# One graph-transformer layer: first loads in another order, query loads placed earlier, other orders in the last group and the last chunk

## What is computed

```python
def _decomp(x, nt, w_comp, w_basis):
    W = (w_comp @ w_basis).reshape(T, x.shape[-1], -1)
    return jnp.einsum('ni,tio->tno', x, W)[nt, jnp.arange(x.shape[0])]
k, q, v = (_decomp(node_feat, node_type, wc, wb).reshape(n, H, DK) for wc, wb in ...)
kt = jnp.einsum('nhi,thij->tnhj', k, relation_att)[edge_type, src]
e = (q[dst] * kt).sum(-1) * relation_pri[edge_type] * scale
m = jax.ops.segment_max(e, dst, num_segments=n)
ex = jnp.exp(e - m[dst])
a = ex / jax.ops.segment_sum(ex, dst, num_segments=n)[dst]
vt = jnp.einsum('nhi,thij->tnhj', v, relation_msg)[edge_type, src]
agg = jax.ops.segment_sum(a[..., None] * vt, dst, num_segments=n).reshape(n, DH)
out = jax.nn.relu(_decomp(agg, node_type, w_comp_a, w_basis_a) + node_feat @ loop_weight + bias)
result = _layernorm(x + out)
```

## Time and profile before

| | us |
|---|---|
| median of 3 runs | 2042.28 |
| the runs | 2038.15 to 2045.23 |
| the profiled execution, its own time | 2054.15 |
| its span, first to last instruction | 2052.3 |
| TensorE busy | 1223.7 |
| VectorE busy | 1005.0 |
| POOL busy | 888.9 |
| ACT busy | 789.1 |

### The profile page before, as it was taken

How to read it: one execution, slowest core, us unless ns; L and a number is a source line. 1 busy time by engine, 2 the same in 40 slices (tenths; PEclk the granted TensorE clock), 3 DMA queues, 4 the chain that set the end, 5 groups by cost and what they waited for, 6 DMA issues and landing times.

```text
span 2052.3 us, 30216 instructions
## 1 busy us (share of the span) xinstructions
PE 1223.7 (60%) x6847; PEld 1015.7 (49%) x6848; DVE 1005.0 (49%) x2888; ACT 789.1 (38%) x2216; POOL 888.9 (43%) x927
## 2 busy tenths in 40 slices
PE   6999428565545555455564565555555455554788
PEld 3445215454445445455454554444544455444678
DVE  5866216444534445344453444434444344453777
ACT  4667216433333333333333333333333333333233
POOL 2781650444454444544445444354443544445000
PEclk9999759666777766777667667667776666667789
DMA  7787530222232222322223222232222322223113
GB/s 228 303 301 313 175 91 12 69 68 75 65 86 73 69 71 63 86 72 67 75 63 85 74 61 77 63 88 67 70 72 65 88 74 61 75 67 85 38 48 106
DMA packets 110628, 194.47 MB, mean 95 GB/s; under 512 B 24345, under 2 KB 76404, under 8 KB 104188
## 3 DMA queue, kind: packets, MB, share of 16 engines
q0 software_dynamic: 41680, 113.71, 19.6%
q1 hardware_dynamic: 66380, 79.10, 11.0%
q10 hardware_dynamic: 2400, 0.07, 0.1%
HBM read 134.12 MB, written 59.48 MB: 94 GB/s over the span
## 4 chain that ended last, share of the span: by engine, by line
another core or an unknown queue 30%; PE 26%; DVE 16%; issue 15%; DVEq 9%; ACT 2%; DMA 1%; ACTq 1%
PE pb L1703 6%; DVE agg L742 5%; PE pb L1651 4%; DVEq L713 4%; PE pb L1538 3%; DVE work L707 3%; PE pb L1813 2%; PE pb L1559 2%; PE pb L1678 2%; PE pb L1609 1%; DVE work L599 1%; PE pb L1640 1%; DVE work L609 1%; DVEq L582 1%
## 5 line engine op out<-in xcount | busy, mean ns | idle before, releaser
L1223 POOL DMA_INDIRECT kv<-table,idx_now x832 | 788.0, 947 | 935.0 <-DVE work L707 645.3
L742 DVE TENSOR_TENSOR agg<-agg,pb 128x136 f32 x832 | 241.8, 291 | 801.5 <-remote 613.8
L1703 PE MATMUL pb<-work,onehot 128*128 128x136 f32 x1664 | 391.6, 377 | 353.4 <-DVE agg L742 225.2
L1703 PEld LDWEIGHTS pb<-work,onehot 128*128 128x128 f32 x1664 | 327.0, 270 | 386.1 <-issue 244.9
L1365 ACT ACTIVATE work<-pb 128x512 f32<-128x512 f32 x208 | 123.9, 596 | 818.9 <-remote 636.6
L1651 PE MATMUL pb<-q_all,work 128*128 x1664 | 313.1, 351 | 0.1
L1651 PEld LDWEIGHTS pb<-q_all,work 128*128 128x128 f32 x1664 | 296.3, 265 | 3.7 <-issue 3.0
L1640 PE MATMUL pb<-ident,onehot 128*128 128x128 f32 x832 | 181.1, 357 | 184.3 <-ACT onehot L1359 99.9
L1352 ACT ACTIVATE work<-lane,neg_lane 128x128 f32<-128x128 f32 x800 | 252.9, 389 | 0.0
L1640 PEld LDWEIGHTS pb<-ident,onehot 128*128 128x128 f32 x832 | 127.6, 184 | 209.6 <-ACT onehot L1359 116.1
L599 DVE TENSOR_TENSOR work<-kv,pb 128x512 f32<-128x512 f32 x208 | 141.9, 682 | 22.0 <-issue 12.0
(11 more groups left out here) (202 smaller groups left out, 1291.4 us busy)
## 6 DMA issues: line engine op xcount, KB each, us to landing
table<-kv SPq DMA_DIRECT2D x49, 1024.0 KB, 4.7
kv<-table,idx_now POOLq DMA_INDIRECT x832
seg<-item_bias SPq DMA_DIRECT2D x52, 64.0 KB
kv<-base_rows SPq DMA_DIRECT2D x7, 448.0 KB, 4.5
kv<-in_x_dram SPq DMA_DIRECT2D x8, 384.0 KB, 5.7
pair<-in_x_dram SPq DMA_DIRECT2D x24, 128.0 KB
base_rows<-pair SPq DMA_DIRECT2D x24, 128.0 KB
onehot<-in_x_dram SPq DMA_DIRECT2D x7, 384.0 KB
```

Source lines behind the costliest of these rows:

```text
L742: v.tensor_tensor(a, a, PB[banks[i // 2 % len(banks)]][:, (i % 2) * 256:(i % 2) * 256 + W], ALU.add).then_inc(s_added, 1)
L1223: pool.indirect_dma_start(out=kv[:, o:o + 2 * D], out_offset=None, in_=table, in_offset=bass.IndirectOffsetOnAxis(ap=idx_now[par][:, i:i + ...
L1703: mm = t_.matmul(PB[banks[k % len(banks)]][:, u * 256:u * 256 + W], onehot[:, o:o + P], wv[:, b % WR, h * 2 + u, :], start=True, stop=True)
```

## The change

- Head: the basis `basis_k` is issued right behind the first chunk of x, `basis_v` as ACT's first transfer. The 8 strips of priorities become one load of all 64 to every partition (`pri_all`), from which VectorE takes each partition's own head by a product with a mask (`own_head`, made by POOL in three steps) and a reduce. POOL copies `src` and `edge_type` only after `dst` has landed and both bases have.
- Table stage: `STARTS_AT` 8 to 9, `COLUMNS_AT` one block later each, `QUERIES_AT` 45 to 41.
- Last group: each step of the maxima ahead of two old additions, and `weigh` in four steps of one item, one behind each addition.
- Last chunk: three parts of 4, 2 and 1 blocks, each with its own residual, statistics, root and reciprocal; ACT normalises the first six blocks and VectorE the last; the output goes in three stores; the last block's product lies in a bank of its own; the root of the chunk before comes one copy earlier on ACT.

```diff
-        TILES_AT, STARTS_AT, BIAS_AT, QUERIES_AT = 4, 8, 24, BLOCKS - 4
-        COLUMNS_AT = [12, 13, 15, 16, 18, 19, 20]
+        TILES_AT, STARTS_AT, BIAS_AT, QUERIES_AT = 4, 9, 24, BLOCKS - 8
+        COLUMNS_AT = [13, 14, 16, 17, 19, 20, 21]
...
-        SPLIT = 4
+        LAST_PARTS = ((0, 4), (4, 6), (6, CB))
...
+        def last_out(c, n):
+            if c == CB - 1:
+                return PB[6][:, 0:D]
+            return PB[4 + c // 4][:, c % 4 * D:(c % 4 + n) * D]
...
             def scale_relations():
-                dve.wait_ge(s_relations_loaded, 16 * 3 * H)
+                dve.wait_ge(s_own_head, 3)
+                dve.wait_ge(s_relations_loaded, 16 * (2 * H + 1))
+                p3 = pri_all.rearrange("p (t h) -> p t h", t=T)
+                did(v.tensor_tensor(p3, p3, own_head.unsqueeze(1).broadcast_to([P, T, H]), ALU.mult))
+                did(v.tensor_reduce(pri, p3, AX.X, ALU.add))
...
+            def weigh_item(g, par, b, u):
+                if u == 0:
+                    dve.wait_ge(s_weights, g * NBATCH + wave_of[b][1] + 1)
+                rows = rows_of(par, b)[:, u, D:2 * D]
+                ins = v.tensor_tensor(wv[:, b % WR, u, 0:D].rearrange("p (h k) -> p h k", h=H),
+                                      rows.rearrange("p (h k) -> p h k", h=H),
+                                      weights_of(b)[:, u, :].unsqueeze(2).broadcast_to([P, H, DK]), ALU.mult)
+                if u == 3:
+                    ins.then_inc(s_weighted, 1)
...
             for k, steps in enumerate(maxima(g, 1, GROUPS // 2 - 1)):
+                steps()
                 late[2 * k]()
                 late[2 * k + 1]()
-                steps()
...
-                merge(adding(g, range(2 * b, 2 * b + 2), LAST_SBANKS), [lambda: weigh(g, 1, b + 2)] if b + 2 < NBATCH else [])
+                merge(adding(g, range(2 * b, 2 * b + 2), LAST_SBANKS),
+                      [lambda u=u: weigh_item(g, 1, b + 2, u) for u in range(4)] if b + 2 < NBATCH else [])
...
+            def finish(ch, par):
+                yl = y[par]
+                for h, (c0, c1) in enumerate(LAST_PARTS):
+                    dve.wait_ge(s_block_multiplied, ch * CB + c1)
+                    o = last_out(c0, c1 - c0)
+                    v.scalar_tensor_tensor(yl[:, c0 * D:c1 * D], o, 0.0, x3[par][:, c0 * D:c1 * D],
+                                           ALU.max, ALU.add).then_inc(s_residual, 1)
...
+                    if h == 0:
+                        turn_round(ch, 0)
+                turn_round(ch, 1)
+                turn_round(ch, 2)
...
             x_chunk(0)
+            sp.dma_start(Bkv[:, :, 0, :], basis_k.rearrange("b (i o) -> i b o", o=D)).then_inc(s_bases_loaded, 16)
             sp.wait_ge(s_setup, mark["comp_zero"])
...
-            for kind, w in enumerate((basis_k, basis_v)):
-                sp.dma_start(Bkv[:, :, kind, :], w.rearrange("b (i o) -> i b o", o=D)).then_inc(s_bases_loaded, 16)
...
-            tile_load(0, dst)
-            tile_load(1, src)
-            tile_load(2, edge_type)
+            tile_load(0, dst, s_tile_rows)
...
-            pool.wait_ge(s_tile_rows, 16 * 8)
+            pool.wait_ge(s_tile_rows, 16 * 4)
             pool.dma_start(tdst, tile_rows.rearrange("(p c) f -> p c f", c=TPR)[:, :, 0:P])\
                 .then_inc(s_tile_dst, 16)
+            pool.wait_ge(s_bases_loaded, 16 * 2)
+            tile_load(1, src, s_tile_more)
+            tile_load(2, edge_type, s_tile_more)
...
+            act.dma_start(Bkv[:, :, 1, :], basis_v.rearrange("b (i o) -> i b o", o=D)).then_inc(s_bases_loaded, 16)
             act.wait_ge(s_setup, mark["comp_zero"])
...
+            act.dma_start(pri_all, rel_pri.rearrange("(a t) h -> a (t h)", a=1).broadcast_to([P, T * H]))\
+                .then_inc(s_relations_loaded, 16)
...
-                with nc.allow_non_contiguous_dma(reason="64 priorities"):
-                    act.dma_start(pri[r, :], rel_pri[:, h:h + 1].rearrange("t a -> a t").broadcast_to([DK, T]))\
-                        .then_inc(s_relations_loaded, 16)
...
-                    if c == 3 and not first:
+                    if c == (2 if final else 3) and not first:
                         deviation(ch - 1)
```

More of the change, by code:

```diff
@@ L173, in graph_transformer_layer @@
         pri = w1.take(T)
+        pri_all = w1.take(T * H)
+        own_head = w1.take(H)
         comp = w1.take(4 * NB, 96)
@@ L1071, in _ @@
             load(CHUNKS - 1, 0)
-            for ch in range(CHUNKS - 3, CHUNKS):
+            for ch in range(CHUNKS - 3, CHUNKS - 1):
                 store(ch)
-            sp.wait_ge(s_stored, 16 * (CHUNKS + 1))
+            ch, c1 = CHUNKS - 1, LAST_PARTS[0][1]
+            oc = yo.rearrange("p (c d) -> p c d", c=CB)
+            sp.wait_ge(s_normalised, ch * CB + c1)
+            sp.dma_start(out[ch * CN:ch * CN + c1 * P, :].rearrange("(c p) d -> p c d", p=P),
+                         oc[:, 0:c1, :]).then_inc(s_stored, 16)
+            sp.wait_ge(s_normalised, ch * CB + LAST_PARTS[1][1])
+            sp.wait_ge(s_last_normalised, 1)
+            sp.dma_start(out[ch * CN + c1 * P:whole * P, :].rearrange("(c p) d -> p c d", p=P),
+                         oc[:, c1:CB - 1, :]).then_inc(s_stored, 16)
+            sp.dma_start(out[whole * P:N, :], oc[0:rest, CB - 1, :]).then_inc(s_stored, 16)
+            sp.wait_ge(s_stored, 16 * (CHUNKS + 2))
         @block.gpsimd
@@ L1460, in deviation, with finish, root, part @@
                 a_.activation(rstd, mv[:, :, 1], ACT.Sqrt, bias=eps[:, 0:1]).then_inc(s_deviation, 1)
+            def finish(ch, par):
+                def root(h):
+                    c0, c1 = LAST_PARTS[h]
+                    act.wait_ge(s_mean_var, ch * CB + c1)
+                    a_.activation(rstd[:, c0:c1], mv[:, c0:c1, 1], ACT.Sqrt, bias=eps[:, 0:1])                        .then_inc(s_deviation, 1)
+                def part(h):
+                    act.wait_ge(s_shift, h + 1)
+                    act.wait_ge(s_stored, ch * 16)
+                    for c in range(*LAST_PARTS[h]):
+                        a_.activation(yo[:, c * D:(c + 1) * D], y[par][:, c * D:(c + 1) * D], ACT.Identity,
+                                      bias=shift[:, c:c + 1], scale=rstd[:, c:c + 1]).then_inc(s_normalised, 1)
+                root(0)
+                part(0)
+                root(1)
+                root(2)
+                part(1)
             def stage3(ch, par, first=False, final=False):
@@ L1477, in _ @@
             stage3(CHUNKS - 1, 0, final=True)
[L1478 to L1483 removed]
+            finish(CHUNKS - 1, 0)
         @block.tensor
```

70 lines of the change are left out of this document (45 added, 25 removed).

## The result

| | before | changed |
|---|---|---|
| median, us | 2043.17 (7 runs) | 2036.03 (7 runs) |
| the runs | 2038.15 to 2046.56 | 2029.32 to 2039.76 |
| ratio | | 0.9962, 95% interval 0.9945 to 0.9979 |
| profiled execution, span | 2052.3 | 2037.1 |

The changed kernel is faster by 7.1 us between the medians, by the interval 4.3 to 11.2 us. The forecast was 13.0, with a range down to 2017 and up to 2041: direction and range hold, and the size is about half. The two profiled spans differ by 15.2, twice the difference of the medians. Much of what follows is about that doubling.

A forecast was written before the change was run, and what follows sets the result against it. The groups loop (1585 of 2052.3 us) was taken as bound by waits around the gathers that the profile can't name, untouched by the change. 3.0 + 4.5 + 2.0 + 1.8 + 1.7 = 13.0 us off 2042.3 gives 2029.3, range 2017 to 2041.

The forecast's parts named there:

- First loads: Head: with both bases issued earlier, first product 3.3 us and scaling 2.8 earlier; 3.0 us taken, between 1.5 and 4.5.
- The scan: Table stage: scan one block later removes TensorE's stall and the lower clock behind it; 4.5 us, between 2.0 and 6.2.
- The query loads: Passage to the query stage: loads issued earlier let the first gather start earlier; 2.0 us, between 0 and 3.3.
- if what it does before the stall is lost by as much: Query stage: case in which an earlier start of the gathers is worth nothing, the lower end of 0 to 3.3.
- The last group: Last group: maxima ahead of old additions and weighing by item, together 1.8 us, between 0.3 and 3.8.
- The weighing: Last group: small weigh steps fit gaps between additions, rounds 2.1 instead of 2.35; 1.5 us over six rounds, at best 3.3.
- the order of the maxima: Last group: maxima steps first, so TensorE's turns run beside old additions; 0.3 us, between 0 and 0.7.
- That rival: Last group: weighing by item costs its durations, 2.6 us lost instead of 1.5 won, giving 2033.4; 12%.
- The last chunk: End: one block left after its product, last normalised block 1.5 us earlier, smaller store; 1.7 us, between 0.9 and 2.3.
- The head's gain is not hidden: Rival, table stage: transfers set the pace and stores catch the head's lead, only 5.5 us stay, 2036.8; 13%.
- The loop did not fall otherwise: Rival, groups: rounds meet the gathers at another moment, one more remote wait in each of 12 passes, 74 us, 2103; 7%.
- The relations did come earlier: Rival, head: message loads or POOL's moved copies delay the relations, the first term falls to 0, 2032.3; 13%.

The follow-up runs named there:

- e11: The kernel before with the scan one block earlier (STARTS_AT 7): 1.0043 to before, 5.9 us over it.
- e7: The changed kernel with the last group's weighing in one step for four items, as before: 0.9958 to the kernel before, 8.7 us under it.
- e10: The kernel before with only the scan and the columns one block later: 0.9995 to before, 0.7 us under it, interval 0.9984 to 1.0007.
- e6: The kernel before with only the query loads four blocks earlier: 0.9990 to before, 2.1 us under it, interval 0.9978 to 1.0002.
- e5: The kernel before against itself, nothing changed, for a second trace: 0.9994, interval 0.9978 to 1.0009.
- e8: The kernel before with only the last chunk in three parts: 0.9991 to before, 1.9 us under it, interval 0.9978 to 1.0003.
- e9: The kernel before with only the reordered first loads: 0.9970 to before, 4.1 us under it.
- e4: The changed kernel with twelve more clears of a node-type buffer ahead of VectorE's first step: 1.0009 to the kernel before, 1.2 us over it.
- e1: The kernel before with the head edits alone (first loads, scan, columns, query loads): 0.9968 to before, 4.4 us under it.
- e3: The changed kernel measured once more, nothing else changed: 0.9939 to the kernel before, 8.4 us under it.
- e2: The kernel before with the edits of last group and last chunk alone: 0.9961 to before, 5.4 us under it.

## Why the prediction was right or wrong

**First loads, 3.0 forecast: 3.5.** The size held, the steps to it only in part, so some of the hit is luck. The step that failed is the delay of the coefficient products behind 512 KB, "which I put at 1 us": it was 2.8, and the first product came 1.9 us earlier in the first pair of traces, not 3.3. In its place the relations gave more than forecast: the wait of 1.52 ahead of the scaling is gone whole, and the terms (they end at 17.81 instead of 19.34) set its start. I had also counted seven transfers less ahead of the last relation; from 22 to 16 it is six.

**The scan, 4.5: about 2.0 in the mean of the traces, and at most 1.0 in four of six executions.** This is the term that failed. The mechanism was read rightly (e11 makes it again and pays 5.5 us; in e7 the late transfer costs nothing). The step that failed is "at 49.67 VectorE has waited 3.67 us": I took the wait of one execution, 3.67, as that of all; it was 1.10, 1.47, 1.79, 1.82 and 3.23 in the other five. As time, the edit alone is not shown at all (e10: 0.7 us, the interval includes zero). The warning stood in my own sum: the profiled execution was 11.9 us above the median, and I subtracted a wait read from it, whole, from the median. The lower bound of the term, 2.0 "if the clock falls all the same", was worked out from the same wait; it should have been the cost where the transfer lands sooner, near 0.

**The query loads, 2.0: 2.2**, and nearly whole, by the traces, on the kind of chip of the first trace, where VectorE hardly moves while the gathers are issued. As time it is not clear of zero (e6: 2.1 us, interval -0.4 to 4.6). The other end of my range, nothing at all, is what the short kind shows. The words "if what it does before the stall is lost by as much" were the right rival.

**The last group, 1.8: about 1.4.** The weighing gives 0.98 of 1.5. I had the rounds right at 2.1, but not their reason: no wait for ACT falls in five of the six, they are 2.0 to 2.1 because the third addition starts 0.51 after the second and the next round's first 0.64 after the fourth (1933.53 to 1934.04, 1934.48 to 1935.12), not 0.44; and the one round that waits for ACT took 2.75. From the first scan (1930.46 and 1919.18) to the first reciprocal it is 31.6 and 30.9, and the 0.65 of the addition that stood ahead of the scan went behind it, 1.4 together. Of this the order of the maxima, forecast at 0.3, gives 0.11; the rest of the 0.4 beside the 0.98 is the longer wait in one round of before, which is not there in every execution (e7 above). The rule of the Trainium skill ("VectorE: DVE Perf Modes", the errata for SBUF sources) on many small tiles did not decide here: the steps are dearer in sum (1.12 against 0.68), as the rule says, but VectorE was idle between dependent additions. That rival is out by e7.

**The last chunk, 1.7: 3.0.** Mis-sized. From the last residual to the last normalised block 2.1 (2031.66 to 2033.77) instead of 4.1; and from the last store's issue to the end 2.9 us (2034.21 to 2037.1) instead of 3.9, where I had expected the 3.9 to stay. The store ahead of it carries 128 KB instead of 384; that this is the reason is not shown by a run of its own. The 3.9 and 2.9 come back in every trace with the old end and with the new.

**The sum.** By the means of all traces it is 3.5 + 2.0 + 2.2 + 1.4 + 3.0 = 12.1, near the forecast of 13.0, because an oversized term and an undersized one meet. On the short kind the scan saves 0.8 (48.5 and 48.0 against 47.5) and the query loads nothing: 8.7 was due, and 8.4 and 9.4 were measured, so the account closes. On the long kind the scan saves 2.5 (50.1 in the mean of four against 47.6), and 12.6 was due, against 7.8 (4.3 to 11.2) on the first chip; for e7, which lacks 1.0 of it, 11.6 against 8.7 (5.6 to 11.8). These sums add terms from single traces, so their own error is not known. By them 3 to 5 us are missing there in the middle, and 0 to 1.4 at the upper ends of the intervals. The loop could hide them: its stretch is 1592.8, 1598.9, 1601.6 and 1598.9 in four traces of one chip (e6, e5, e8, e7), with the same loop in all four. Whether it was longer in the mean after the change can't be told from one trace for each kernel. That stays open.

**The doubling.** 15.2 us between the two profiled spans and 7.1 between the medians, 8.1 too many. The profiled execution of the kernel before lies 11.0 above its median of seven, that of the changed kernel 2.9 above its own. Most of it is in the head: against e5, the first trace of before is 6.6 us later at the first gather (5.1 between blocks 2 and 16, 2.6 behind them, 1.1 less ahead).

**The rivals.** The head's gain is not hidden behind the stores (e9: 4.1 us for the first loads alone). The loop did not fall otherwise by tens of us: no trace shows it, and a start 6 us later (e4) did not shorten it. The relations did come earlier.

**The signs.** Seen as forecast: the scaling at 18.2, no wait of the scan, no stretch at 0.50 behind it, rounds of 2.1. The first gather is 13.5 us earlier in the first pair, and 10.4 in the mean of the long kind (212.1 in before, e5 and e8, 201.7 in the changed kernel and e7). Not as forecast: the first product at 12.9, between my right and my wrong, and in e1, e3 and e7 above 13, my sign of being wrong; and 2.9 us behind the last store instead of 3.9. The length of the groups stretch could not serve as a sign: the kernel before has 1572.0 and 1598.9 on two chips of one kind.

## What to carry to other kernels

Before a wait for a transfer becomes a term of a sum, look whether the profiled execution is longer than the median; if it is, the wait may be the excess, and its lower bound is zero. The reverse is no safeguard: in e8, 1.6 us above its median, the wait is 3.23. Trace the same kernel a second time: that showed more here than most of the single edits did. Where a chain of dependent steps leaves gaps on an engine, work cut into pieces that fit the gaps can pay even if the pieces are dearer in sum, as 0.98 us did here. And moving transfers earlier pays only as far as the next thing that their user waits for: the same edit was worth 2 us on one chip and nothing on another.

## What was not expected of the hardware

Some chips run the kernel before in 2043 and 2078 us, others in 1380. The durations of POOL's and VectorE's instructions agree (a gather 0.947 and 0.950 us, VectorE busy 1007.5 and 1004.4 in the changed kernel); what differs are the waits around the gathers and the register steps, on VectorE at most 1386 to 1424 ns on the long kind and 110 ns on the short. TensorE is busy longer on the long kind, 1228.3 us against 1063.2, at a mean granted clock of 0.737 against 0.865. And a wait of 3 to 4 us for a transfer of the side work costs more than itself: where TensorE idled 2.71 (e8), 3.16 and 4.26 us, its granted clock behind was 0.75, 0.50 and 0.72 in the mean of 6.1 us; where it idled 0.95, 1.27 (e9) and 1.30 (e2), it was 1.00.
